# A two-layer graph network: gathered rows in a ring of eight groups, four gathers a step behind a TensorE signal

## What is computed

```python
agg = segment_sum(weight[:, None] * x[src], dst)
x = layernorm(x + relu((x + agg) @ W1 + b1) @ W2 + b2)
agg = x
for _ in range(3):                       # three hops, head = src, tail = dst
    h, t = agg[head], agg[tail]
    att = sum((h @ q_w) * tanh(rel * t @ k_w), axis=1)      # rel = edge_emb[type]
    w = softmax of att over the edges of a head
    summed = segment_sum(w[:, None] * rel * t, head)
    agg = summed / max(count, 1), divided by its norm
    out = out + agg + x
x = layernorm(x + out)
```

## Time and profile before

| | |
|---|---|
| median of 3 runs | 14879.7 us (14873.69 to 14883.93) |
| span of the profiled execution | 14895.7 us |
| TensorE matmuls busy | 9009.4 us, 60% |
| TensorE weight loads busy | 6806.5 us, 46% |
| VectorE busy | 6224.1 us, 42% |
| ScalarE busy | 6149.7 us, 41% |
| GpSimd busy | 6417.6 us, 43% |
| mean granted TensorE clock | 0.725 |
| HBM over the span | 72 GB/s |

### The profile page before, as it was taken

How to read it: one execution, slowest core, us unless ns; L and a number is a source line. 1 busy time by engine, 2 the same in 40 slices (tenths; PEclk the granted TensorE clock), 3 DMA queues, 4 the chain that set the end, 5 groups by cost and what they waited for, 6 DMA issues and landing times. The chain is left out here.

```text
span 14895.7 us, 251017 instructions
## 1 busy us (share of the span) xinstructions
PE 9009.4 (60%) x47197; PEld 6806.5 (46%) x47197; DVE 6224.1 (42%) x27880; ACT 6149.7 (41%) x15788; POOL 6417.6 (43%) x6756
## 2 busy tenths in 40 slices
PE   2465555566777777777755555555555556555665
PEld 2343443444555555555544444444444444444444
DVE  3555555565333333333343333333334333333334
ACT  1355555553333333333334444444443444444443
POOL 4554554442444434444334444444434444444443
PEclk7566666667777777777777777777777777777777
DMA  2111111112444444444433333333343333333333
GB/s 63 37 37 34 36 35 35 33 35 77 127 125 126 125 125 126 125 125 126 124 102 105 106 104 106 104 105 101 108 99 105 104 104 107 102 105 105 109 109 93
DMA packets 1390477, 1399.81 MB, mean 94 GB/s; under 512 B 239512, under 2 KB 1066681, under 8 KB 1390137
## 3 DMA queue, kind: packets, MB, share of 16 engines
q1 hardware_dynamic: 1173398, 951.42, 21.2%
q0 software_dynamic: 216064, 444.28, 12.3%
q10 hardware_dynamic: 876, 2.56, 0.1%
HBM read 888.87 MB, written 183.76 MB: 72 GB/s over the span
## 5 line engine op out<-in xcount | busy, mean ns | idle before, releaser
L621 POOL DMA_INDIRECT tails<-node_rows,idx x4992 | 4732.3, 948 | 6564.6 <-ACT idx L649 5017.2
L1753 DVE SCALAR_TENSOR_TENSOR acc<-acc,fade,banks 128x129 f32 x4992 | 1718.4, 344 | 5486.8 <-remote 3164.9
L1838 PE MATMUL banks<-rt,weight_t 128*128 128x129 f32 x9984 | 1783.3, 335 | 1486.3 <-issue 802.1
L1838 PEld LDWEIGHTS banks<-rt,weight_t 128*128 128x128 f32 x9984 | 1607.8, 244 | 1631.4 <-issue 1206.6
L621 POOL DMA_INDIRECT l_rows<-in_x_dram,l_idx x1664 | 1585.1, 953 | 1529.5 <-ACT l_idx L649 1017.3
L1846 ACT ACTIVATE weight_t<-banks 128x512 f32<-128x512 f32 x1248 | 745.5, 597 | 3569.1 <-remote 2286.4
L1825 PE MATMUL banks<-ident,weight 128*128 128x128 f32 x4992 | 1070.4, 353 | 1878.0 <-ACT weight L1866 1767.1
L1818 PE MATMUL banks<-right,window 128*128 128x128 f32 x9984 | 1774.8, 335 | 459.9 <-issue 459.2
L1818 PEld LDWEIGHTS banks<-right,window 128*128 128x128 f32 x9984 | 1590.2, 242 | 538.2 <-issue 510.7
L1829 PE MATMUL banks<-rtt,k_sb 128*128 128x512 f32 x2496 | 1741.3, 789 | 1.4 <-ACT rtt L1853 1.4
L1825 PEld LDWEIGHTS banks<-ident,weight 128*128 128x128 f32 x4992 | 752.0, 181 | 2041.5 <-ACT weight L1866 1931.4
(11 more groups left out here) (309 smaller groups left out, 9792.2 us busy)
## 6 DMA issues: line engine op xcount, KB each, us to landing
window<-qt SPq DMA_DIRECT2D x4992, 64.0 KB
rel<-rel_kept SPq DMA_DIRECT2D x832, 256.0 KB
rows_in<-tile_rows SPq DMA_DIRECT2D x416, 256.0 KB
rel_kept<-rel SPq DMA_DIRECT2D x416, 256.0 KB
mask<-mask_kept SPq DMA_DIRECT2D x832, 128.0 KB
tails<-node_rows,idx POOLq DMA_INDIRECT x4992
mask_kept<-mask SPq DMA_DIRECT2D x416, 128.0 KB
l_rows<-in_x_dram,l_idx POOLq DMA_INDIRECT x1664
```

Of the source, the lines that this page charges most:

```text
L621: e.indirect_dma_start(out=rows[:, g, t % GROUP, :], out_offset=None, in_=of, in_offset=bass.IndirectOffsetOnAxis(ap=idx[:, b, t:t + 1], a ...
L1753: e.scalar_tensor_tensor(to, to, fade[:, g2, t:t + 1], bank[b_acc + t // 2][:, t % 2 * WIDE:t % 2 * WIDE + WIDE], ALU.mult, ALU.add).then_ ...
L1838: mm = e.matmul(bank[b_acc + t // 2][:, t % 2 * WIDE:t % 2 * WIDE + WIDE], weight_t[:, s.slot(4, 2), t, :], rt[:, s.slot(4, UNROLL), t, :] ...
```

## The change

The ring of gathered rows has eight groups in place of four, in layer 0 and in the hops, and `idx` has four batches in place of two. ScalarE copies, at step i, the indices of groups i+6 and i+7. GpSimd gathers group by group, four gathers at a time. For group g it waits for the slot (`rt` or `l_weighed` of g-8), for the indices where g is even, and for a TensorE signal: in the hops `s_rtt` with value g-4, which is given in step g-4, in layer 0 `s_acc` with value g-5, given in step g-4 too. The first five groups of a hop (six in layer 0) wait for no such signal.

Slots of the ring are now found by constants only if a loop body has eight steps, so all pipelines but the ones for nodes go in turns of eight (`TURN`). The index tables get four more groups at their end. To make room, `turned` is laid over `rtt`, and the four semaphores of the query stage are those of an earlier stage.

```diff
-RING = 4
+RING = 8
+TURN = 8
...
-        def pool_rows(e, name, rows, idx, of, s_free):
-
-            def batch(b):
-                for t in range(BATCH * GROUP):
-                    g = b * BATCH + t // GROUP
-                    e.indirect_dma_start(out=rows[:, g, t % GROUP, :], out_offset=None, in_=of,
-                                         in_offset=bass.IndirectOffsetOnAxis(ap=idx[:, b, t:t + 1], axis=0)).then_inc(sp_tail[g].h, 16)
-
-            for b in range(2):
-                e.wait_ge(s_copy_idx.h, s_copy_idx.at(b + 1))
-                batch(b)
...
-            with e.Fori(0, z.slot_groups // BATCH // 2 - 1):
-                for b in range(2):
-                    e.wait_ge(s_free.h, s_free.at(BATCH))
+        def pool_rows(e, name, rows, idx, of, s_free, s_step, behind):
+
+            def gather(g):
+                b, first = g // BATCH, g % BATCH * GROUP
+                for t in range(GROUP):
+                    e.indirect_dma_start(out=rows[:, g, t, :], out_offset=None, in_=of,
+                                         in_offset=bass.IndirectOffsetOnAxis(ap=idx[:, b, first + t:first + t + 1], axis=0)).then_inc(sp_tail[g].h, 16)
+
+            for g in range(RING):
+                if g % BATCH == 0:
+                    e.wait_ge(s_copy_idx.h, s_copy_idx.at(g // BATCH + 1))
+                if g > behind:
+                    e.wait_ge(s_step.h, s_step.at(g - behind))
+                gather(g)
...
+            e.reg_mov(stepped, s_step.at(RING - behind))
+            with e.Fori(0, z.slot_groups // RING - 1):
+                for g in range(RING):
+                    e.wait_ge(s_free.h, s_free.at(1))
                     e.wait_ge(s_free.h, freed)
-                    e.wait_ge(s_copy_idx.h, copied)
-                    batch(b)
-                    e.reg_add(freed, freed, BATCH)
-                    e.reg_add(copied, copied, 1)
...
+                    if g % BATCH == 0:
+                        e.wait_ge(s_copy_idx.h, copied)
+                    e.wait_ge(s_step.h, stepped)
+                    gather(g)
+                    e.reg_add(freed, freed, 1)
+                    e.reg_add(stepped, stepped, 1)
+                    if g % BATCH == 0:
+                        e.reg_add(copied, copied, 1)
...
-            for b in range(2):
+            for b in range(RING // BATCH):
                 e.activation(idx[:, b, :], others[:, b * BATCH * GROUP:(b + 1) * BATCH * GROUP], ACT.Copy).then_inc(s_copy_idx.h, 1)
...
                 s.wait_ge((s_free, done(1)))
-                s.e.activation(idx[:, (s.i // BATCH + 1) % 2, :], others[:, bass.ds(s.at(lambda i: GROUP * (i + BATCH)), BATCH * GROUP)], ACT.Copy)\
+                s.e.activation(idx[:, (s.i // BATCH - 1) % (RING // BATCH), :], others[:, bass.ds(s.at(lambda i: GROUP * (i + RING - BATCH)), BATCH * GROUP)], ACT.Copy)\
                     .then_inc(s_copy_idx.h, 1)
...
-                    pool_rows(e, "l0", rows, idx, x, s_rt)
+                    pool_rows(e, "l0", rows, idx, x, s_rt, s_acc, 5)
...
-                    phases(e, "gt", tensor_l0, z.slot_groups, steps, (UNROLL, GROUP * UNROLL))
+                    phases(e, "gt", tensor_l0, z.slot_groups, steps, (TURN, GROUP * TURN), TURN)
...
-        s_qturn, s_qturned, s_q, s_qt = (sem(f"q_s_{n}") for n in ("turn", "turned", "q", "qt"))
+        s_qturn, s_qturned, s_q, s_qt = s_turn, s_turned, s_w1, s_hidden
...
-                turned = tensor(ctx, f"turned{hop}", [P, 2, BANK])
+                turned = rtt
...
-                        g4, g8 = s.slot(1, UNROLL), s.slot(1, UNROLL)
+                        g4, g8 = s.slot(1, UNROLL), s.slot(1, RING)
...
-                        pool_rows(e, f"hop{hop}", tails, idx, node_rows, s_rt)
+                        pool_rows(e, f"hop{hop}", tails, idx, node_rows, s_rt, s_rtt, 4)
...
-                        pipeline(e, f"he{hop}", tensor_hop, z.slot_groups, deep, (UNROLL, GROUP * UNROLL, 16 * GROUP))
+                        pipeline(e, f"he{hop}", tensor_hop, z.slot_groups, deep, (TURN, GROUP * TURN, 32 * GROUP), TURN)
```

More of the change, by code:

```diff
@@ new lines, in pool_rows @@
+        def pool_rows(e, name, rows, idx, of, s_free, s_step, behind):
[10 more added lines that the diff above has]
+                gather(g)
+            freed, copied, stepped = (e.alloc_register(f"{n}_{name}") for n in ("freed", "copied", "stepped"))
+            e.reg_mov(freed, s_free.at(1))
+            e.reg_mov(copied, s_copy_idx.at(RING // BATCH + 1))
+            e.reg_mov(stepped, s_step.at(RING - behind))
+            with e.Fori(0, z.slot_groups // RING - 1):
+                for g in range(RING):
+                    e.wait_ge(s_free.h, s_free.at(1))
+                    e.wait_ge(s_free.h, freed)
+                    if g % BATCH == 0:
[6 more added lines that the diff above has]
+                        e.reg_add(copied, copied, 1)
+            for r in (freed, copied, stepped):
+                e.free_register(r)
@@ L723, in _ @@
                         e.tensor_tensor(pay[:, 1, :], type_at[:, :], lower[:, :], ALU.add)
-            others = tensor(ctx, "l0_others", [P, z.slot_tiles + BATCH * GROUP], I32)
+            others = tensor(ctx, "l0_others", [P, z.slot_tiles + (RING - BATCH) * GROUP], I32)
             weights = tensor(ctx, "l0_weights", [P, z.slot_tiles])
@@ L1027, in gnn_two_layers @@
             inner = ExitStack()
-            idx = tensor(inner, "l0_idx", [P, 2, BATCH * GROUP], I32)
+            idx = tensor(inner, "l0_idx", [P, RING // BATCH, BATCH * GROUP], I32)
             rows = tensor(inner, "l0_rows", [P, RING, GROUP, z.D])
@@ L1426, in _ @@
                     first_idx(e, others, idx)
-                    phases(e, "ga", scalar_l0, z.slot_groups, steps, (UNROLL, 16 * GROUP))
+                    phases(e, "ga", scalar_l0, z.slot_groups, steps, (TURN, 16 * GROUP), TURN)
                 @block.vector
@@ L1434, in _ @@
                     e.wait_ge(s_column.h, 1)
-                    phases(e, "gv", vector_l0, z.slot_groups, steps, (UNROLL, GROUP * UNROLL))
+                    phases(e, "gv", vector_l0, z.slot_groups, steps, (TURN, GROUP * TURN), TURN)
                     e.wait_ge(s_taken.h, z.slot_tiles)
@@ L1532, in gnn_two_layers @@
             s_stored.base += 48
-        others = tensor(top, "tails_of_slots", [P, z.slot_tiles + BATCH * GROUP], I32)
+            for s in (s_turn, s_turned, s_w1, s_hidden):
+                s.base += node_groups
+        others = tensor(top, "tails_of_slots", [P, z.slot_tiles + (RING - BATCH) * GROUP], I32)
         parted = tensor(top, "parted", [P, z.slot_tiles])
@@ L1698, in gnn_two_layers @@
                 qt = tensor(ctx, f"qt{hop}", [P, z.NP])
-                idx = tensor(ctx, f"idx{hop}", [P, 2, BATCH * GROUP], I32)
+                idx = tensor(ctx, f"idx{hop}", [P, RING // BATCH, BATCH * GROUP], I32)
                 tails = tensor(ctx, f"tails{hop}", [P, RING, GROUP, z.D])
@@ L1955, in _ @@
                         e.wait_ge(s_qt.h, s_qt.at(node_groups))
-                        pipeline(e, f"hs{hop}", sync_hop, z.slot_groups, deep, (UNROLL,) if first else (UNROLL, GROUP * UNROLL))
+                        pipeline(e, f"hs{hop}", sync_hop, z.slot_groups, deep, (TURN,) if first else (TURN, GROUP * TURN), TURN)
                         if first:
@@ L1972, in _ @@
                         vector_q(e)
-                        pipeline(e, f"hd{hop}", vector_hop, z.slot_groups, deep, (UNROLL, 2 * UNROLL, GROUP * UNROLL, 16 * GROUP, 32))
+                        pipeline(e, f"hd{hop}", vector_hop, z.slot_groups, deep, (TURN, 2 * TURN, GROUP * TURN, 16 * GROUP), TURN)
                         vector_nodes(e)
@@ L1984, in _ @@
                         scalar_q(e)
-                        pipeline(e, f"ha{hop}", scalar_hop, z.slot_groups, deep, (UNROLL, GROUP * UNROLL, 32))
+                        pipeline(e, f"ha{hop}", scalar_hop, z.slot_groups, deep, (TURN, GROUP * TURN, 64), TURN)
                         scalar_nodes(e)
-                s_copy_idx.base += z.slot_groups // BATCH + 1
+                s_copy_idx.base += (z.slot_groups + RING) // BATCH - 1
                 for s in (s_oht, s_rel, s_copied) if first else (s_copied,):
```

7 lines of the change are left out of this document (1 added, 6 removed).

## The result

The changed kernel takes 12,508.9 us (median of 4 runs, 12,507.2 to 12,532.8); the kernel before took 14,881.8 us on the same chip. The ratio is 0.8415, with a 95% interval of 0.8401 to 0.8428. The forecast was 13,680 us with a range of 12,950 to 14,910: the direction was right, but the gain of 2,373 us was twice the 1,200 that I had worked out. The profiled executions lie 2,390 us apart (14,895.7 and 12,505.4), and the stages account for it.

What follows compares the result with a forecast made beforehand. TensorE signals held during gather bursts were taken to bound the kernel. Hop steps of 8.4, 7.7 and 7.7 us save 1223 us: 14895.7 - 1223 + 10 + 15 = 13698, less 16 us: 13,680 us, range 12,950 to 14,910.

Steps and rivals of the forecast that it cites:

- The lever: TensorE's signals are held until a burst of gathers ends, so bursts of four in place of eight shorten the holds.
- The period of 7.5 us: Step with one burst of four: 3.75 us first to last start, release 3.0 later, next burst 0.77 after that.
- The reaction of 0.77: Time from release of the transposes' signal to POOL's next burst, read in the quiet step: 0.77 us.
- TensorE's clock: Hop steps: 0.25 x 0.7 us added to 7.5 in hops 1 and 2, giving 7.7; hop 0 taken at 8.4.
- Layer 0: No step under 7.5 us when each has its own burst: +10 us, bounds 300 us less or more.
- Costed at nothing: POOL's added waits, index copies, loops of eight steps and SyncE's window loads: all expected to be covered, 0 us.
- rival B: Another limit takes over, SyncE or a misplaced hold: hop steps of 9.0, 8.4, 8.4 us, total 14,510 us; 12%.
- The starts and ends of stages: At each hop's start five groups are gathered at once in place of four: +15 us over three hops.
- A: Hold follows the gathers, not the burst, 0.6 us each wherever it stands: nothing won, 14,900 us; 8%.
- C: Eight-step loop bodies are fetched anew each turn, 2.0 us each, uncovered: +306 us, 13,990 us; 5%.
- D: Work after a release is not hidden: 2.0 us left in the hops, steps of 9.5 us, total 15,630 us; 15%.
- What the profile would show: Four gathers once a step, even steps near 7.7 us, longest hop "remote" waits from 7 to 9 us to under 5.

Runs made afterwards that it cites:

- e2: Kernel after, but at every second group POOL waits for two groups' slots and signals, then starts all eight gathers: 14,670 us, ratio 0.9841.
- e20: Kernel after with both signals moved: hops wait for the et transposes, layer 0 for TensorE's signal one step later; 11,991 us, ratio 0.8163.
- e9: Kernel after, but in layer 0 POOL does not wait for TensorE's signal: 12,844 us, layer 0 at 3,051 us.
- e1: Kernel before with its loops run in turns of eight steps, ring and bursts as before: 14,902 us, ratio 1.0007.
- e14: Kernel after, unchanged, run again in a session where signals are not held: 9,129 us, ratio 0.9955.
- e7: Kernel after, but in the hops POOL waits for the et transposes (of weight) instead of the rt transposes: 11,991 us.
- e6: Kernel after, but in the hops POOL waits for VectorE's rt product instead of the rt transposes: 13,048 us.
- e8: Kernel after, but in the hops POOL waits for the acc matmuls, TensorE's last group of the step: 12,546 us.
- e18: Hop 0 gathers as in the kernel after, hop 1 loads fixed rows on GpSimd's queue, hop 2 on SyncE's: steps 7.98, 4.73 and 6.20 us.
- e11: Plain loads of fixed rows, issued by GpSimd, in a session where signals are not held: 8,721 us.

## Why the prediction was right or wrong

*The lever* was right: TensorE's signals are held until a burst is over, and the change makes bursts shorter. e2 gives the gain in the hops back by making them long again. The two sizes that hung on it were wrong, and both fell on the same side: 727 us in the hops (9,877 forecast, 9,150 measured) and 477 in layer 0.

*The period of 7.5 us* was the step that failed, and in it the release. I had 3.75 + 3.0 + 0.77, with 3.0 read in the earlier trace rows behind a burst of eight. Behind four it is 2.28, and the tail is no constant: 2.04, 2.27, 2.38 and 2.90 us behind three, four, five and eight. 0.7 us in 1,245 steps are 870 us. The reaction of 0.77 was sound in hops 1 and 2 (0.86 in the cycle above). In hop 0 it is 2.03 at the median, since `rt` and its transposes are left behind the release: 1.3 us a step more than my sum had. A coarser reading would have come a little nearer in hops 1 and 2: the long step of 11.42 us, less four gathers of 1.25, is 6.4.

*TensorE's clock.* The trace gives the granted clock as a share of full speed, and in the kernel before it is 0.5 or 1.0 throughout, in 780 stretches each. The two levels that the line over the earlier trace rows names are these (1.00 over 8010 to 8015 us, 0.50 over 8058.8 to 8061); no run gives them as frequencies. The sum has 0.25 x 0.7 = 0.2 us a step for the lower level in hops 1 and 2, and in hop 0 0.9 us, which make 8.4 of 7.5. Both were my estimates and no run shows these terms; what the runs showed in their place is 0.08 us and none. The measured 6.97 is 0.08 over the 6.89 of the cycle, with the mean granted clock at 0.87 against 0.76 before. In hop 0 7.96 came. That near hit is luck: the cycle there is 3.75 + 2.28 + 2.03 = 8.06 without any share for the clock, so a release put too long and a clock term that is not needed made up for the work left behind the release. What a slow matmul in the middle of a hold costs, no run tests. A gap ahead of a group does not go with slow matmuls in every step: the acc matmuls at 8004.47 come behind 2.12 us of idle time, and the att matmuls right after them, at 8005.47, took 1.06 us, as in the earlier trace rows, with a granted clock of 1.00 over both. Over hop 2, 35% of the matmuls of either group took over 0.41 us each; the median is 0.42 at a granted clock of 0.5 and 0.27 at 1.0.

*Layer 0* was the other miss: +10 us forecast, bounds of 300, and -467 measured. The sentence that failed is "a step cannot go under 7.5 when each has its own burst". Steps there do not have their own bursts: bursts are of eight, mostly, and of four, and what went were the sixteens. That the eights arise because two signals come out together at a release is my reading; e20's later signal left them as they were, as it should by this reading. I had seen them in the earlier trace rows (a wait of 14.30 us) and did not price what would cut them. e9 shows that it is the signal.

*Costed at nothing:* the loops (e1: right, but for the fetches), the copies of indices, the waits on POOL (e14's gathers above stay 1.25 us apart through them), the rows' lead. SyncE's four window loads take about 2.4 us at the median in hops 0 and 2, and they did before as well (in hop 1 2.99 against 2.44): the 3.54 of the earlier trace rows was not typical, and rival B had little to rest on. The starts and ends of stages cost 26 us, 15 were forecast.

*The rivals.* A (the hold follows the number of gathers) is refuted by the steps of e2 beside the kernel after: as many gathers, 8.90 and 6.97 us. B did not come. C came true in one hop of three. Hop 1 takes 0.15 us a step more than hop 2, 63 us in place of 306, and part of that may be other work. D (work left after the release) is hop 0's case, with 1.2 us a step and not 2.0, under the 1.9 us from which it would have lost there; it is not that of hops 1 and 2.

*What the profile would show:* bursts of four once a step and even steps were right. "The longest remote waits under 5 us" was not; hop 1 has them up to 6.7 us, and 8.7 for `acc`, and the steps are shorter all the same. What fell is their number on the two paths of the earlier trace rows, from 147 to 32 for `acc` and from 150 to 13 for `rtt`.

*What I could not know* from one trace: in some sessions nothing is held, and there the same change is worth 0.5% and not 16%. The prediction is one for the kind in which its trace was taken.

## What to carry to other kernels

Where a trace has waits put down as "remote", find what is in flight when they end, and count them from the last of it, at the length that the changed kernel will have. Place the work that needs no signal inside the hold and the trigger of the next burst at the first signal that is let go; moving one wait by two groups of matmuls was worth another 3% (e7). After moving a trigger, count the bursts that come out, since they can merge (e6, e8). And before tuning around such a wait, time both kernels in another session, on another chip if there is one.

## What was not expected of the hardware

- The hold is there in some sessions and not in others. In the session of the result and in four others TensorE's signals are held beside indexed gathers, in two they are not, with the same instructions at the same 1.25 us pace: 14,882 and 12,509 us against 9,168 and 9,129. What differs between the two kinds no run here can show; the number of one chip came up in a session of either kind.
- Gathers with an index per row hold; plain loads of neighbouring rows from the same queue, as many and as large, do not (e18).
- It is TensorE's signals that are late, 1,268 of 1,719 in hop 2 of the kernel after, and none of the 5,037 of VectorE and ScalarE.
- The release comes 2.04 us after the last gather's start behind a burst of three and 2.90 behind eight.
- Without a hold GpSimd's issue of gathers is the bound, 4 x 1.25 us a step, and with plain loads (0.53 us each) the hops fall to 4.4 to 5.2 us a step and the kernel to 8,721 us (e11).
